# Silu visits ahead of the other ScalarE work of their place, four normalisations four places later, and D·u by way of ScalarE and transpositions

## The reference

```
xz = x @ win.T
u, z = jnp.split(xz, 2, axis=-1)
...
u = jax.nn.silu(jnp.transpose(uc, (0, 2, 1)) + bconv)
dbc = u @ wx.T
...
delta = jax.nn.softplus(dt @ wdt.T + bdt)
dA = jnp.exp(delta[..., None] * A)
dBu = (delta * u)[..., None] * Bm[:, :, None, :]

def step(h, t):
    dA_t, dBu_t, C_t = t
    h = dA_t * h + dBu_t
    return (h, jnp.einsum('bdn,bn->bd', h, C_t))
...
y = jnp.swapaxes(ys, 0, 1) + u * Dp
y = y * jax.nn.silu(z)
return y @ wout.T
```

## Time and profile before

| | us |
|---|---|
| median of 3 runs | 7538.63 (7533.7 to 7550.31) |
| the profiled execution | 7541.42, its span 7539.2 |
| POOL busy | 6962.0 (92% of the span) |
| PE busy | 6812.2 (90%) |
| DVE busy | 6774.4 (90%) |
| ACT busy | 6182.2 (82%) |
| DMA engines' share, q1 | 48.1% |
| granted PE clock, mean | 0.975 of full speed |

### The profile page before, as it was taken

How to read it: one execution, slowest core, us unless ns; L and a number is a source line. 1 busy time by engine, 2 the same in 40 slices (tenths; PEclk the granted TensorE clock), 3 DMA queues, 4 the chain that set the end, 5 groups by cost and what they waited for, 6 DMA issues and landing times. The chain is left out here.

```text
span 7539.2 us, 111379 instructions
## 1 busy us (share of the span) xinstructions
PE 6812.2 (90%) x32682; PEld 4023.5 (53%) x32682; DVE 6774.4 (90%) x9064; ACT 6182.2 (82%) x13081; POOL 6962.0 (92%) x3774
## 2 busy tenths in 40 slices
PE   6899988999999999999999999999989999999889
PEld 3455555555555555555555555555555555555455
DVE  2799999999999999999999999999999999999766
ACT  1788888888888888888888888888888888888745
POOL 0899999999999999999999999999999999999678
PEclk8999999999999999999999999999999999999999
DMA  7544455444444454444444544444455444444555
GB/s 255 147 137 133 132 142 150 112 138 140 138 133 129 141 151 116 133 140 137 133 131 141 150 118 131 141 138 133 128 142 151 113 135 141 138 133 129 159 185 173
DMA packets 605402, 1064.06 MB, mean 141 GB/s; under 512 B 113584, under 2 KB 221872, under 8 KB 596336
## 3 DMA queue, kind: packets, MB, share of 16 engines
q1 hardware_dynamic: 602704, 1055.81, 48.1%
q10 hardware_dynamic: 2080, 1.05, 0.0%
HBM read 926.59 MB, written 130.03 MB: 140 GB/s over the span
## 5 line engine op out<-in xcount | busy, mean ns | idle before, releaser
L691 POOL TENSOR_TENSOR dBu<-Bb,du 128x1024 f32<-128x1024 f32 x2048 | 4793.9, 2363 | 3.4 <-DMA Bb<-bc_scratch 3.3
L806 ACT ACTIVATE scans<-delta,A 128x512 f32<-128x512 f32 x4096 | 2766.5, 693 | 409.2 <-DVE hC L1159 337.5
L1143 DVE TENSOR_TENSOR_SCAN scans<-scans,state,dBu 128x512 f32<-128x512 f32 x2016 | 2540.2, 1281 | 332.5 <-ACT scans L806 332.5
L1143 DVE TENSOR_TENSOR_SCAN dBu<-scans,state,dBu 128x512 f32<-128x512 f32 x1568 | 1962.5, 1264 | 13.5 <-ACT scans L806 10.6
L1016 PE MATMUL yT<-ident,hC 128*128 128x128 f32 x9216 | 1398.0, 282 | 302.6 <-DVE hC L1159 301.1
L1159 DVE TENSOR_TENSOR hC<-scans,Cb 128x512 f32<-128x512 f32 x2304 | 1560.2, 682 | 1.1 <-PE yT L1016 1.1
L701 POOL TENSOR_TENSOR hR<-dBu,Cb 128x512 f32<-128x512 f32 x1024 | 1304.5, 1274 | 205.5 <-DVE dBu L1143 204.9
L1016 PEld LDWEIGHTS yT<-ident,hC 128*128 128x128 f32 x9216 | 1065.0, 144 | 625.5 <-DVE hC L1159 405.4
L1009 PE MATMUL bg<-u,comb 128*128 128x512 f32 x2112 | 989.4, 594 | 1.1 <-DVE u L1124 0.9
L948 PE MATMUL bg<-hT,win_u 128*128 128x512 f32 x2112 | 967.4, 598 | 0.9 <-ACT hT L728 0.9
L970 PE MATMUL bg<-hT,win_z 128*128 128x512 f32 x2048 | 963.3, 593 | 0.0
(11 more groups left out here) (161 smaller groups left out, 7891.4 us busy)
## 6 DMA issues: line engine op xcount, KB each, us to landing
comb<-pre_scratch SPq DMA_DIRECT2D x1040, 256.0 KB, 4.6
Bb<-bc_scratch SPq DMA_DIRECT2D x264, 512.0 KB, 7.0
Cb<-bc_scratch SPq DMA_DIRECT2D x264, 512.0 KB, 7.0
win_u<-in_win SPq DMA_DIRECT2D x264, 256.0 KB, 4.6
pre_scratch<-pre SPq DMA_DIRECT2D x264, 256.0 KB, 3.8
comb<-comb_scratch SPq DMA_DIRECT2D x66, 1024.0 KB, 8.6
win_z<-in_win SPq DMA_DIRECT2D x257, 256.0 KB, 2.8
part_scratch<-pre SPq DMA_DIRECT2D x132, 256.0 KB, 2.0
```

The lines of the kernel that those rows point to most:

```text
L691: pool.tensor_tensor(dBu[:, ring(g, q)], Bb[:, 2 * q:2 * q + 2, :], du[:, j % 2, :].unsqueeze(1).broadcast_to([P, 2, T]), ALU.mult).then_i ...
L806: act.activation(place(n)[:], delta[:, j % 2, :], ACT.Exp, scale=A[:, i % 2, j * N + n:j * N + n + 1]).then_inc(dA_made, 1)
L1143: nc.vector.tensor_tensor_scan(to, place(n)[:], dBu[:, ring(g, q), k, :], state[:, c:c + 1] if i % CH_SEQ else 0.0, ALU.mult, ALU.add).the ...
```

## The change

Three things are changed; the mathematics stays.

1. **Visits.** At a place in `GATED` the visit now comes right behind the two decays and ahead of the evictions and normalisations of that place. The condition on the table becomes strict for C, since a Silu may no longer use an eviction of its own place.
2. **Normalisations.** `NORM_POS` goes from 50 to 54: they stand at the places 54 to 57.
3. **D·u.** The diagonal matrices, their store and their loads go. ACT multiplies u by D itself, 128x512 into a new tile `su`, at q = 2 of every tile between the two decays; PE adds `su` to `yT` at q = 3 by four transpositions as it does with the states. `turn_back` has no product any more. With it, `CT` keeps only the three columns of C that are used.

```diff
-NORM_POS = 50
+NORM_POS = 54
...
-                sp.dma_start(skip[:, j % 2], dram["skip"][d, j]).then_inc(sk_loaded[j % 2], 16)
...
                         keep_state(g, j, 2 * q - KEPT_BEHIND)
+                        if q == SKIP_AT - 1:
+                            act.wait_ge(su_used, g)
+                            act.mul(su[:], u[:, s, j, :], skip[:, i // CH_DIR, j:j + 1]).then_inc(su_made, 1)
                         if q == 1:
...
                         step_dA(g, i, j, 2 * q + 1)
                         keep_state(g, j, 2 * q + 1 - KEPT_BEHIND)
+                        if p in GATED:
+                            nc.scalar.preload_act_table_set(SILU)
+                            for kind, k in GATED[p]:
+                                if kind == "C":
+                                    silu_u(freed(i, f"C{k + 1}"), k, 2, 1 - s)
+                                else:
+                                    silu_z(freed(i, f"Z{k}"))
+                            nc.scalar.preload_act_table_set(EXP_LN)
                         if p == 12:
...
                             if p == NORM_POS + tt:
                                 normalize(i + 2, tt, cur)
-                        if p in GATED:
...
-            def turn_back(bank, g, j, s, loads, taken):
-                pe.wait_ge(sk_loaded[j % 2], loads)
-                nc.tensor.matmul(bank[:], skip[:, j % 2, :], u[:, s, j, :], start=True, stop=True,
-                                 skip_group_check=True)
+            def turn_back(bank, g, taken):
                 pe.wait_ge(bg_free, taken)
...
+                        if q == SKIP_AT:
+                            pe.wait_ge(su_made, g + 1)
+                            add_state(su[:], False).then_inc(su_used, 1)
```

More of the change, by code:

```diff
@@ L104 @@
          47: (("C", 4), ("Z", 5)), 52: (("C", 6), ("Z", 6)), 63: (("Z", 7),)}
-assert all(TAKE[f"{kind}{m + (kind == 'C')}"] <= p and (kind == "C" or p // NQ == m) for p in GATED for kind, m in GATED[p])
+assert all(TAKE[f"{kind}{m + (kind == 'C')}"] < p + (kind == "Z") and (kind == "C" or p // NQ == m) for p in GATED for kind, m in GATED[p])
 assert sorted(m for p in GATED for kind, m in GATED[p] if kind == "C") == list(range(0, MT, 2))
@@ L236, in _ @@
             act.mul(alog[:], alog[:], -1.0).then_inc(alog_made, 1)
-            act.wait_ge(ident_made, 2)
-            for d in range(2):
-                for m in range(MT):
-                    ins = act.mul(skip_diag[:, d, m, :], ident[:], skip[:, d, m:m + 1])
-                ins.then_inc(skip_made, 1)
-                act.wait_ge(skip_made, d + 1)
-                act.dma_start(dram["skip"][d].rearrange("m p c -> p m c"), skip_diag[:, d]).then_inc(skip_stored, 16)
-            act.wait_ge(skip_stored, 32)
             act.wait_ge(flip_made, 2)
@@ L559, in _ @@
             load_x("x", 0)
+            sp.dma_start(skip[:], io["Dp"]).then_inc(sk_loaded, 16)
             sp.dma_start(modt[:], dram["modt"][:, 0:2, :]).then_inc(modt_loaded, 16)
@@ L571, in _ @@
             load_z(0, 0)
-            sp.dma_start(skip[:, 1], dram["skip"][0, 7]).then_inc(sk_loaded[1], 16)
             sp.wait_ge(consts_made, 2)
@@ L1026, in turn_back @@
                     for tt in range(TT):
-                        nc.tensor.matmul(bank[:, tt * P:(tt + 1) * P], turned[:, k, tt * P:(tt + 1) * P], ident[:], start=False,
-                                         stop=False, is_transpose=True, skip_group_check=True)
+                        nc.tensor.matmul(bank[:, tt * P:(tt + 1) * P], turned[:, k, tt * P:(tt + 1) * P], ident[:],
+                                         start=k == 0 and tt == 0, stop=False, is_transpose=True, skip_group_check=True)
                 pe.wait_ge(yT_taken, g + 2)
```

40 lines of the change are left out of this document (15 added, 25 removed).

## The result

The changed kernel is slower. Its median is 7592.24 us over six runs (7571.35 to 7596.63), against 7538.18 for six runs of the kernel before (7533.7 to 7550.31), taken beside them: a ratio of 1.0064, 95% interval 1.0051 to 1.0078, which is 38 to 59 us. Forecast were 7465 us and a range up to 7560; the direction was wrong too. The profiled execution took 7591.07 us.

The account below looks back on a forecast made before the run. ACT's decays feeding DVE's scans were taken to bound the kernel. Per chunk, place 23 -1.3, place 31 +1.1 and places 47 to 53 -2.1 made -2.3 us, times 32 = -74: 7465 us against 7538.63, range 7395 to 7560.

Parts of the forecast that it names:

- places 47 to 53: ACT's unbroken row in tile 6: wait ahead of C6 and three normalisations go, `yt` limits; -2.1 us per chunk.
- D·u: ACT's product at q = 2 covered except in tile 6, +0.6 us per chunk; PE net -0.45 per tile.
- place 23: Visit starts 1.60 us earlier, so does tile 3's first scan; PE hands back part; -1.3 us per chunk, bounds 0.8 and 1.6.
- place 31: U3's later eviction makes PE stand 3.8 us at D5, partly regained; +1.1 us per chunk, bounds 0.3 and 3.8.
- place 15: Wait of 0.77 us ahead of the visit goes, but PE has no idle time in tiles 1 and 2; counted 0.
- The rival that ACT's product isn't covered: ACT's product with D, 8 x 0.6 us per chunk, shows in full; +67 us, 7608; chance 0.04.
- The rival sentence beside it: Slow transpositions cost PE 0.69 us per tile more; three tiles passing it on make 2.1 per chunk, 7532; no own chance.
- the stall at 48: Sign: DVE's scan stall at place 48 falls to about 1 us, while the one at 53 stays near 3.
- the new wait at D5: Sign: PE newly waits 3 to 4 us at D5 for ACT's eviction `pre`.
- The sign that was to show the forecast wrong: DVE's stalls on decays don't fall by about 2 us per chunk, or fall while the chunk doesn't shorten.
- `hR`'s waits: Sign: POOL's waits at `hR` for DVE's scans fall from 204.9 us to about 130 over the run.
- bank waits decide: Rival: PE's waits at D5 (place 31) and O3 (place 15) cost 3.8 + 1.0 us per chunk; 7586; chance 0.13.

Follow-up runs that it names:

- e15: Kernel before, with the visit ahead of the evictions at place 47 alone and the normalisations at 54 to 57; 7463.57 us (0.9881).
- e1: Changed kernel, with the visit at place 31 alone put back behind the evictions; 7485.75 us (0.9922).
- e9: Kernel before, with visits ahead of the evictions at all places but 31 and normalisations at 54 to 57, D·u made as before; 7470.44 us (0.991).
- e10: Changed kernel, with 40 transpositions of a tile of zeros on PE ahead of D5's wait for its bank; 7508.52 us (0.9958).
- e3: Changed kernel, with five products of a tile of zeros on PE ahead of D5's wait for its bank; 7520.59 us (0.9969).
- e7: Kernel before, with the visit ahead of the evictions at place 23 alone; 7542.86 us (0.9998).
- e14: Kernel before, with half of tile 3's projection of z left out and the visit ahead of the evictions at place 23; 7518.2 us (0.9956).
- e12: Kernel before, with one more ACT product per tile at q = 2, into a tile that nobody reads; 7550.71 us (1.0011).
- e13: Kernel before, with half of tile 3's projection of z (two of four products, place 25) left out; 7559.25 us (1.0015).
- e16: e9 with 28 transpositions of zeros on PE ahead of C6's wait for its data; 7463.11 us (0.9886).
- e4: Changed kernel, with D5 one place later in the table (32 for 31); 7636.8 us (1.0112).

## Why the prediction was wrong

The sum can be set against the runs term by term, in us of the whole run. Each measured term is the difference of two kernels that differ in that step, one after the other from the kernel before to the changed one, so the column adds up by its making. The interval of each kernel is some 10 us wide to either side; +15 and +12 are not clear of it.

| step | on record | measured | from |
|---|---|---|---|
| places 47 to 53, without the product with D | -86 | -85 | e15 |
| D·u (the product of tile 6 alone on record) | +19 | +15 | e1 against e9 |
| place 23 and the other visits but 31 and 47 | -42 | +12 | e9 against e15 |
| place 31 | +35 | +112 | after against e1 |
| sum | -74 | +54 | |

**The step that failed most is place 31.** "Bounds 0.3 (all but the `yt` hidden) and 3.8 (nothing got back); I take 1.1." The wait was seen, its place and nearly its size: 3.8 forecast, 4.68 in chunk 10. What was missing is that this wait of PE is followed by products at half the clock, 77 to 89 us of the 112. What passes from the wait itself is 23 to 35 us, by e10 and e3 against e1, and that this meets the 1.1 per chunk on record (35) is luck: that value was worked out over the z of tile 4, and ACT waits 0.71 us for that z in the changed kernel, as it did (0.72). The sentence "ACT's own later `yt` costs no more than the same stretch" is where it came in: `yt` is a wait of ACT in the middle of a row of decays, it ends with PE's last products of the tile, and those came at 2505.99, 5.9 us after the first decay of tile 4. In the kernel before they ended with it, at 2480.58 for 2480.56. Three decays of lead are used up by that, and DVE stands 2.05 us at the fourth. The step followed PE's queue to z and compared it with the idle rows there; it should have followed it to `yt` first, which is nearer. That the term's upper bound (3.8 per chunk) held the measured 3.5 is no merit, as it counted no clock and the value was taken from nearer the other end.

**Place 23** was the second. "PE stays behind by then and hands back part": it hands back all. The prediction counted PE's idle rows at 32 and 33 as a sign that PE has room in tile 3; those lie behind the eviction of U3 and the turned states, for which ACT waits. e7 shows nothing kept, e14 0.9 to 1.3 us once PE has less to do. For place 15, one tile earlier, the same reasoning was used and gave 0; no run has that place alone, but in the changed kernel ACT stands 1.58 us ahead of the next `yt` for PE.

**D·u** came out near its size for a wrong reason. "Net -0.45 per tile": PE's busy time did fall, by 78 us in e1 (6678.7) against e9 (6756.7), where 0.45 in each of 256 tiles had been 115. But the product removed stood in part in the shadow of the wait for `yt`, and the transpositions stand where PE is late. Alone it is +53. The rival that ACT's product isn't covered was rightly held small: e12, +7. The rival sentence beside it, that three PE-bound tiles could pass the cost on, was nearer, though not by slow transpositions: they take 0.11 us each here.

**Places 47 to 53** was right in size and, in e15, in its mechanism, and the two edits belong together: alone they gave 22 and 31, not 85. The forecast that the stall at 48 shrinks to about 1 us held (0.85); that the one at 53 stays near 3 did not (1.55, and 2.27 in e15).

Of the signs named beforehand: no wait ahead of the table loads at 23 and 47, the new wait at D5 (4.68 for 3 to 4 us) and no wait of PE for `su` came as forecast. `yt` of tile 6 doesn't wait for PE in chunk 10 of the changed kernel (it does in e15), and the wait for tile 4's z is no longer than it was. The sign that was to show the forecast wrong came: DVE's stalls on decays did not fall by 2 us in the chunk, they went from 11.5 to 11.7. `hR`'s waits did not fall to about 130: 249.2. They do in e1 (133.4), e9 (126.3) and e15 (127.8).

The rival "bank waits decide" had 7586 us, near the 7592 measured, but by another sum: O3 does wait 1.0 us per chunk as it said (32.2 us in all, also in e1 and e9, which are faster than the kernel before), and D5's wait by itself passes on 0.7 to 1.1, not 3.8. Two slips stand in the sums: 8 x 0.6 is 4.8 and not 5.0, and most of the rivals were added to 7541, the profiled execution, where the forecast goes down to the median; neither is over 10 us.

What stays open: why D·u costs 53 us alone and 15 in company, how much of e13's time is the lower clock, and the part of the changed kernel's last 27 us that is not in DVE's busy time.

The best kernel that was run is e15, 7463.57 us (0.9881): the visit ahead of the evictions at place 47 only, and the normalisations at 54. e9 and e16 are not told apart from it by more than their intervals.

## What to carry to other kernels

The wait that this edit gave to TensorE had two prices: what stands behind it in its queue, and the half clock in which it was then worked off. Look in the granted clock of the windows at what earlier waits of that length were followed by (here C6's, in the trace of before), and if the wait can't be avoided, fill it. When an eviction is put behind something, follow the next user of its bank to the nearest thing that any engine on the critical chain waits for, not the largest idle gap. A microsecond taken off the engine that is waited for counts only if no other engine is late in the same tile; try such edits one by one, since of the eight visits moved here one gave something (47), one took back more than that (31), and the others gave nothing together. And a run that leaves work out can have a new wait, and a lower clock behind it (e13), so look at its trace before it is used as a base.

## What the runs showed of the hardware

- After PE stood 4.68 us, the granted clock was 0.50 for the next 3.80 us (1.2 GHz) and 0.85 in the 3.00 us after that. D5 took 2.07 for 1.12, C2 1.94 for 1.06. Over 32 chunks this was 77 us (e3) or 89 us (e10) of 7592.
- In e4 PE waited 1.28 us ahead of 2511.28 and 1.89 ahead of 2517.01; the granted clock was 1.00 from 2515 to 2517, 0.57 from 2517 to 2521 and 0.50 from 2521 to 2525. In e13 a wait of 1.84 us, ahead of 2469.99, was followed by 0.52 from 2471 to 2474.5.
- Forty fp32 transpositions of a 128x64 tile (into 64 partitions) took 4.53 us, 0.11 each, and the granted clock behind them was 1.00, as behind products (e3).
- Work that adds zeros can make a kernel quicker: e10 has 40 transpositions per chunk more than the changed kernel, and takes about 1% less time (0.9958 against 1.0064).
